# Conv, rank and attention kernel on one core: attention weights on TensorE, two-lane sort, and new written-out orders

## The reference

```python
corr = jnp.einsum('bmc,bnc->bmn', x3, x3) / c
x_sort = jnp.sort(corr, axis=-1)[..., ::-1]
x = x + x_sort[..., ranks]
for window in (4, 16, 32):
    attn = softmax(einsum(q, keys) * scale)
    contexts.append(einsum('blw,blwd->bld', attn, values))
t = t + hidden + (sum(contexts) / 3) @ Wo + bo
```

## Time and profile before

| | |
|---|---|
| time, median of 3 | 4914.16 us (4904.6 to 4914.23) |
| profiled execution, own time | 4910.64 us |
| its span, first to last instruction | 4908.8 us |
| VectorE (DVE) busy | 87% |
| TensorE (PE) busy | 81% |
| ScalarE (ACT) busy | 60% |
| GpSimd (POOL) busy | 18% |
| mean granted TensorE clock | 0.896 of 2.4 GHz |

### The profile page before, as it was taken

How to read it: one execution, slowest core, us unless ns; L and a number is a source line. 1 busy time by engine, 2 the same in 40 slices (tenths; PEclk the granted TensorE clock), 3 DMA queues, 4 the chain that set the end, 5 groups by cost and what they waited for, 6 DMA issues and landing times.

```text
span 4908.8 us, 56286 instructions
## 1 busy us (share of the span) xinstructions
PE 3958.7 (81%) x19410; PEld 2667.5 (54%) x19410; DVE 4267.6 (87%) x5380; ACT 2954.4 (60%) x7241; POOL 884.1 (18%) x580
## 2 busy tenths in 40 slices
PE   5747748889798988989798988989798987867587
PEld 3616424567456654567456654567456654545354
DVE  1098999999999999999999999999999999999521
ACT  4526526687467846687467846677467845554452
POOL 2316000242005300242005300242005300000000
PEclk8878869999799998999799988999799998988798
DMA  4314100232013210232013210232013210010001
GB/s 132 98 35 123 37 0 18 67 105 63 16 43 110 79 36 18 71 104 65 11 43 110 79 36 18 71 102 63 14 44 110 77 34 16 20 30 27 10 24 37
DMA packets 226037, 269.28 MB, mean 55 GB/s; under 512 B 26831, under 2 KB 188506, under 8 KB 225626
## 3 DMA queue, kind: packets, MB, share of 16 engines
q0 software_dynamic: 46080, 151.03, 10.6%
q1 hardware_dynamic: 179674, 114.65, 8.0%
HBM read 242.25 MB, written 23.34 MB: 54 GB/s over the span
## 4 chain that ended last, share of the span: by engine, by line
DVE 41%; PE 36%; ACT 9%; issue 6%; POOL 4%; DMA 4%; SPq 1%; DVEq 0%; POOLq 0%; ACTq 0%
PE bank L597 5%; POOL gath L759 4%; PE bank L1298 3%; PE bank L1633 3%; PE bank L1628 3%; DMA gath<-quads,idx 3%; PE bank L1613 3%; DVE srt_b L794 3%; DVE srt_b L881 3%; DVE srt_b L796 3%; DVE srt_a L893 2%; DVE srt_b L873 2%; DVE srt_a L794 2%; DVE srt_a L796 2%; PE bank L569 2%
## 5 line engine op out<-in xcount | busy, mean ns | idle before, releaser
L759 POOL DMA_INDIRECT gath<-quads,idx x576 | 883.9, 1535 | 3075.4 <-DVE idx L722 1990.3
L597 PE MATMUL bank<-diag,gath 128*128 128x128 f32 x4608 | 615.0, 296 | 168.5 <-DMA gath<-quads,idx 168.5
L639 ACT ACTIVATE diag<-ident,w 128x128 f32<-128x128 f32 x2304 | 704.7, 393 | 30.7 <-DVE w L737 21.2
L597 PEld LDWEIGHTS bank<-diag,gath 128*128 128x128 f32 x4608 | 593.8, 211 | 203.9 <-DMA gath<-quads,idx 187.6
L1613 PEld LDWEIGHTS bank<-e2w,act 128*128 128x128 f32 (+1 forms) x3072 | 408.0, 198 | 161.3 <-issue 156.7
L1628 PE MATMUL bank<-mu_t,e2w 128*128 128x512 f32 (+1 forms) x768 | 421.9, 632 | 82.4 <-DMA e2w<-moe_w_t 36.2
L1633 PE MATMUL bank<-gated_u,e2w 128*128 128x512 f32 (+1 forms) x768 | 426.2, 638 | 36.7 <-DVE act L1713 32.9
L1713 DVE TENSOR_TENSOR act<-act,bank 128x512 f32<-128x512 f32 (+1 forms) x384 | 261.0, 680 | 183.6 <-PE bank L1633 160.8
L1613 PE MATMUL bank<-e2w,act 128*128 128x128 f32 (+1 forms) x3072 | 413.2, 281 | 1.6 <-DVE act L1713 1.6
L1681 ACT ACTIVATE act<-bank 128x512 f32<-128x512 f32 (+1 forms) x384 | 227.6, 593 | 208.6 <-PE bank L1628 206.0
L873 DVE TENSOR_TENSOR srt_b<-srt_a 128x1024 f32<-128x1024 f32 x192 | 350.9, 1828 | 1.5 <-issue 0.3
(11 more groups left out here) (348 smaller groups left out, 8134.4 us busy)
## 6 DMA issues: line engine op xcount, KB each, us to landing
e2w<-moe_w_t SPq DMA_DIRECT2D x256, 170.5 KB
quads<-xn_tok SPq DMA_DIRECT2D x256, 64.0 KB
e1w<-L_ffn_w SPq DMA_DIRECT2D x256, 64.0 KB, 1.9
e2w<-moe_w_t SPq DMA_DIRECT2D x256, 64.0 KB
gath<-quads,idx POOLq DMA_INDIRECT x576
e2w<-moe_w_t SPq DMA_DIRECT2D x128, 42.5 KB
x_tok<-x SPq DMA_DIRECT2D x8, 512.0 KB, 4.4
out<-tm SPq DMA_DIRECT2D x16, 256.0 KB, 2.5
```

Source lines behind the costliest of these rows:

```text
L597: ins = T.matmul(FB[q % 2][:, k * P:(k + 1) * P], gath[:, g % 2, k, s * C:(s + 1) * C], diag[:, g % 2, 4 * k + s], start=(s == 0), stop=(s ...
L639: ins = SC.activation(diag[:, g % 2, n], ident[:], ACT.Copy, scale=w[:, n:n + 1])
L759: pool.indirect_dma_start(gath[:, g % 2, k], None, quads, bass.IndirectOffsetOnAxis(idx[:, TG * g + k:TG * g + k + 1], 0)).then_inc(sem["g ...
```

## The change

- `prob` goes. VectorE takes the reciprocals only. ScalarE builds twelve diagonals `pdiag` (identity scaled by a reciprocal) for a unit, and TensorE multiplies each window's `sm` with its diagonal, three windows into one bank; this transposes and weights at once. The keys of the tile before (32 of them) now lie on partitions 0 to 31, so their values are computed once more on 32 partitions (`v_past`).
- The sort pairs token j with j + 512 and works on two interleaved lanes of 512; each lane has merges of m = 8 (four to a lane) to 1024, all at distance 2 or more, and the last, bitonic merge takes lane 0 against lane 1 backwards. `places` goes. `corr_used` is set after the first full layer.
- The three bias rows are loaded broadcast to 128 partitions and added with the identity as weights.
- The quads are stored in 16 DMAs of 128 KB, each from 32 partitions with the token column as the slowest dimension, once both halves of `xn_tok` are there.
- The order strings of all kinds but `fill` are new. VectorE's letters are the same in number (228 S, 14 F, 36 C in `early`); ScalarE has 2 and TensorE 1 C letter more for each C unit.

```diff
     DVE_early=(
-        "SSSSSSSSSSSSSSSSSSSSSSSSSSSSSSFFSSFSSFSSSSSSSSSSSSSSSFSSSFSSFFSSFSSSSSSSSSSSSSSSSSSSSSSSSSSSSSSS"
-        "SSSSSSSSSSSSSSSSSSSSSSSSSSSCSSCSSSSSSSSSSCCSSCCSSSSSFSSCFSSCFSSFSSSFCSSCSSCSSCSSCSSSCSSSSSSSSSSS"
-        "SSSSCSSCSSSSSSSSSSSCCSSCSSCSSCSSCCSSCSSCSSCSSSSSCSSSSCCSSSSCCSSSSCCSSSSCSSCSSCSSSSSSSS"
+        "SSSSSSSSSSSSSSSSFFSSSFSSFSSSSSSSSSSSSSSSFSSSFSSFFSSFSSSSSSSSSSSSSSSSSSSSSSSSSSSSSSSSSSSSSSSSSSSS"
+        "SSSSSSSSSSSSSSSSSSSSSSSSSSSSSCSSCSSSSSSSSCCSSCSSCSSSSSSSSSSSSCFFSSCFSSFSSCFCSSCSSSCSSCSSCSSSSSSS"
+        "SSSSSSSSSSCSSCSSSSSSSSSSSCSSCSSCSSCSSCSSSCCSSCSSCSSCSSSSCSSSSCCSSSSCCSSSSCCSSSSCSSCSSC"
     ),
...
     PE_full=(
...
-        "MCMCCCCCCCCMCMCMMMMFMMMFMFMMCMMMMFCMMMMMMCFCCFCCFFCCFCFCCFFFFFFFFFFFF"
...
+        "MMCMFMMMFMMFMCMMMFMCMMMFMMMCMMMFCCMMMFFCCMMMFCCMFMFMMMFCMMMFCMMMCMMFFFF"
...
     DVE_full=(
-        "MCMSSCSSMSSSSMSSCCMSSCCMSSMSSMSSSCSSCMSSMSSCMCSSSCMCSSCMCSSMSSSSSSSMSSSSSSSSCMFFCMSSFSSSFSSSSCSS"
...
+        "MCSSCMSSSSSSSMSSSCCMSSCCMSSMSSSMSSMSSSSCSSSCMSSMSSCMCFCFCSSCMCFSSMSSSSSMSSFSSSSSSMSSSSSMSSMSSCSS"
...
             x_in=16, x_t=4, xt_sb=4, gn_mom=4, gn_avg=4, gn_std=2, gn_scale=2, gn_out=6, xn_back=2, xn_tok=2,
-            om_done=2, om_t=2, om_ps=1, om_sb=1, sig=1, quad_out=16 * 32, idx=1, w4=1,
+            om_done=2, om_t=2, om_ps=1, om_sb=1, sig=1, quad_out=16 * 16, idx=1, w4=1,
             gath0=16 * TG * NG // 2, gath1=16 * TG * NG // 2, diag=NG, colt=NG, cols=NG, conv=NT, x1=NT,
-            corr_mm=24, corr_sb=16, sd=1, absd=8, x2_copy=1, out0=16, out1=16, dve_F=17, dve_C0=53, dve_C1=54)
+            corr_mm=24, corr_sb=16, sd=1, absd=8, x2_copy=1, out0=16, out1=16, dve_F=17, dve_C0=47, dve_C1=48)
...
             load(conv_w[:], A["L0_conv_kernel"].rearrange("(t c) f -> c t f", c=C))
-            load(conv_bias[:], A["L0_conv_bias"].rearrange("a b c f -> (a b c) f"))
+            load(conv_bias[:], A["L0_conv_bias"].rearrange("a b c f -> (a b c f)").partition_broadcast(P))
...
         def sp_F(sp, i):
             q = quads.rearrange("(y x) (s c) -> y x s c", x=CELL, c=C)
-            for t in range(NT):
-                if t % 4 == 0:
-                    sp.wait_ge(sem["xn_tok"], img("xn_tok", i, t // 4 + 1))
-                    settle(sp)
...
-                for dy in range(2):
-                    for dx in range(2):
-                        there = q[ROWS * t + 1 - dy:ROWS * t + 1 - dy + ROWS, 1 - dx:1 - dx + WIDTH, 2 * dy + dx]
-                        sp.dma_start(there, xn_tok[:, t]).then_inc(sem["quad_out"], 16)
-                if t % 4 == 3:
-                    yield
+            sp.wait_ge(sem["xn_tok"], img("xn_tok", i, 2))
+            settle(sp)
+            sp.wait_ge(sem["gath0"], img("gath0", i, 0))
+            settle(sp)
+            sp.wait_ge(sem["gath1"], img("gath1", i, 0))
+            settle(sp)
+            for dy in range(2):
+                for dx in range(2):
+                    for r in range(ROWS):
+                        there = q[r + 1 - dy:r + 2 - dy + HEIGHT - ROWS:ROWS, 1 - dx:1 - dx + WIDTH, 2 * dy + dx]
+                        sp.dma_start(there.rearrange("t x c -> x t c"),
+                                     xn_tok[WIDTH * r:WIDTH * (r + 1)]).then_inc(sem["quad_out"], 16)
+                yield
 
...
                     T.matmul(out, ident[:], x_tok[:, t], start=True, stop=False)
-                    T.matmul(out, ones[0:1, :], conv_bias[:], start=False, stop=False)
+                    T.matmul(out, ident[:], conv_bias[:], start=False, stop=False)
                     for k in range(TAPS):
...
                 yield
-                there = corr[:, t % UT].rearrange("p (s k r) -> p s k r", k=2, r=P)
+                there = corr[:, t % UT].rearrange("p (b k w) -> p b k w", k=2, w=2)
-                    SC.activation(there[:, :, k], FB[1 - k][:].rearrange("p (s r) -> p s r", r=P), ACT.Identity,
+                    SC.activation(there[:, :, k], FB[1 - k][:].rearrange("p (b w) -> p b w", w=2), ACT.Identity,
                                   scale=0.5 / C).then_inc(sem["corr_sb"], 1)
                     yield
...
                 lo, hi = src[:, :, 0:size // 2], src[:, :, size // 2:size]
-                if size == TOK:
-                    hi = hi[:, :, ::-1]
 
-            def places(buf):
-                return buf[:].rearrange("p g (s r) -> p g s r", s=8)
...
-
-                V.tensor_tensor(out_lo, lo, hi, ALU.max)
-                yield
-                link.put(V.tensor_tensor(out_hi, lo, hi, ALU.min))
-                yield
-                link.wait()
...
-            m = 16
-            while m < TOK:
-                first = m == 16
-                if not first:
+            ins = yield from compare(8, runs(corr, 8), runs(srt_a, 8))
+            ins.then_inc(sem["corr_used"], 1)
+            yield
+            dve.wait_ge(sem["corr_used"], unit("corr_used", i, h))
+            now = 0
+            m = 8
+            while m <= TOK:
+                if m > 8:
                     link.wait()
-                ins = yield from compare(m, runs(corr if first else bufs[now], m), runs(bufs[1 - now], m))
-                if first:
-                    ins.then_inc(sem["corr_used"], 1)
-                else:
+                    ins = yield from compare(m, runs(bufs[now], m), runs(bufs[1 - now], m))
                     link.put(ins)
-                yield
-                if first:
-                    dve.wait_ge(sem["corr_used"], unit("corr_used", i, h))
-                now = 1 - now
+                    yield
+                    now = 1 - now
                 here, there = runs(bufs[now], m), runs(bufs[1 - now], m)
 
...
                 k = m // 4
-                while k >= 1:
+                while k >= 2:
                     lo, hi = pairs(here, k)
                     out_lo, out_hi = pairs(there, k)
                     link.wait()
                     V.tensor_tensor(out_lo, lo, hi, ALU.max)
                     yield
-                    if k == 1:
-
-                        V.tensor_copy(edges(there, 0, 1), edges(here, 0, 1))
+                    if m == 8:
+
+                        link.put(V.tensor_tensor(hi, lo, hi, ALU.min))
+                        yield
+                        link.wait()
+                        link.put(V.tensor_copy(lo, out_lo))
+                        yield
+                        break
+                    if k == 2:
+
+                        V.tensor_copy(edges(there, 0, 2), edges(here, 0, 2))
                     elif k < m // 4:
 
                         V.tensor_copy(edges(there, 1, k // 2), edges(here, 1, k // 2))
                     link.put(V.tensor_tensor(out_hi, lo, hi, ALU.min))
                     yield
-                    if k == 1:
+                    if k == 2:
                         now = 1 - now
                         break
...
 
-            k = TOK
+            pair = bufs[now][:].rearrange("p g (j w) -> p g j w", w=2)
+            lo, hi = pair[:, :, :, 0], pair[:, :, ::-1, 1]
+            half = bufs[1 - now][:].rearrange("p g (w j) -> p g w j", w=2)
+            link.wait()
+            V.tensor_tensor(half[:, :, 0], lo, hi, ALU.max)
+            yield
+            link.put(V.tensor_tensor(half[:, :, 1], lo, hi, ALU.min))
+            yield
+            now = 1 - now
+            k = TOK // 2
...
             yield
+            pe.wait_ge(sem["qkv_sb"], unit("qkv_sb", i, h, 3))
+            for t in range(UT):
+                ins = T.matmul(CB[0][0:BACK, t * P:(t + 1) * P], utile(t)[:, P - BACK:P], wqkvo[:, 2], start=True, stop=True)
+            ins.then_inc(sem["qkv"], 1)
+            yield
             pe.wait_ge(sem["qkv_sb"], unit("qkv_sb", i, h, 2))
             for p in range(2):
                 for t in range(2):
@@ -1030,27 +1009,28 @@
             for p in range(2):
                 pe.wait_ge(sem["probd"], unit("probd", i, h, p + 1))
                 if p == 0:
-                    pe.wait_ge(sem["prob_z"], unit("prob_z", i, h))
-                    pe.wait_ge(sem["qkv_sb"], unit("qkv_sb", i, h, 3))
-                for t in range(2):
-                    for s in range(2):
-                        ins = T.transpose(CB[p][:, (2 * t + s) * P:(2 * t + s + 1) * P], prob[:, 2 * p + t, s * P:(s + 1) * P], ident[:])
+                    pe.wait_ge(sem["qkv_sb"], unit("qkv_sb", i, h))
+                for t in range(2 * p, 2 * p + 2):
+                    for k, n, at in ((0, BACK, 0), (BACK, P, P)):
+                        for w in range(NW):
+                            ins = T.matmul(CB[p][0:n, t % 2 * 2 * P + at:t % 2 * 2 * P + at + P], sm[:, t, w, k:k + n],
+                                           pdiag[:, t * NW + w], start=(w == 0), stop=(w == NW - 1))
                 ins.then_inc(sem["prob_ps"], 1)
                 yield
...
                     out = CB[2][:, t * P:(t + 1) * P]
-                    past = v_tok[:, t - 1] if t else v_halo[:]
```

(39 more changed lines are left out.)

141 lines of the change are left out of this document (55 added, 86 removed).

## The result

The changed kernel takes 4735.3 us (median of 4 runs, 4731.7 to 4740.5) against 4910.8 for the kernel before on the same chip: ratio 0.9648, 95% interval 0.9636 to 0.966.

What follows compares the result with a forecast made beforehand. VectorE was taken to set the pace except in fill and drain. From 4910.64: fill -4, early body -17, six full bodies and the late one -78.4, drain +5, together -94.4: 4816, stated as 4818 us; range 4775 to 4870.

Steps and rivals of the forecast that it cites:

- A row on one partition costs 0.32 us, its neighbour on 128 partitions 0.31: nothing either way: TensorE's bias matmuls: moving the rows from one to 128 partitions was claimed to change nothing in the time.
- I give the other new orders no gain and no loss: Order strings in the full bodies: an earlier start of F hides behind VectorE, the other new orders change nothing.
- shortens the time by about that much: Bodies 0 to 7: a microsecond taken from VectorE saves about a microsecond, as long as nobody else becomes late.
- slack for 5 us: Full bodies: the attention chain, some 5 us a unit longer, costs nothing, as two C units share 550 us.
- The rival of shorter waits: VectorE's waits in seven bodies: the orders shorten them by 6 us each, 42 more, giving 4776; chance 0.12.
- What hides TensorE's 9.0 is its own idle time: Attention on TensorE: 9.0 us added work an image, mostly hidden; 1.6 us an image charged, bounds 0 and 9.0.
- Drain, +5: Drain: the longer attention chain has no slack there and adds 5 us, bounds 0 and 8.
- VectorE's work: VectorE, per image: sort saves 2.6 us a unit and attention 3.8, together 12.8 us.
- no price for lanes: Sort's last merge: step-of-two reads are free; the rival had 3.3 us more a unit, 4871, chance 0.05.
- Fill: Fill: fewer stores let the first gather go earlier, -5.5, bias rows' loads +1.5; -4, bounds -5.5 and +2.
- late correlations: Rival at seven image borders: new orders make the sort wait for `corr`, 162 us in, 4986; chance 0.06.
- the prediction's other case: Fill's stores: if SBUF ports limit, they take 45 us and the fill is 22 us longer, a sum of 4843.

## Why the prediction was wrong, and where it was right

**The step that failed: "A row on one partition costs 0.32 us, its neighbour on 128 partitions 0.31: nothing either way".** The two means of the earlier trace rows don't hold the price, because it shows in when the matmuls around it start. The runs put 72 us in its place (44 under the old orders): 0.37 to 0.39 us a matmul, 7.1 us of TensorE a full body, 9.4 us of the body. Without it the number would have been near: the changed kernel with the bias rows undone takes 4807 us, where 4818 was said for a term of nothing (own range 4795 to 4840). The comparison with `x_tok` could not warn: its mean is 291 ns in the changed kernel with the rows on 128 partitions and on one, while the bias matmul's goes from 275 to 321 and the eighteen behind it from 275 to 283. It should have gone from start to start, against a matmul of the same columns that has only neighbours of 128 partitions.

**"I give the other new orders no gain and no loss".** That the rest of the sum came out near is luck: two steps of it were wrong by far more than the 11 us that were left. Undoing the orders costs 214 us; under the old strings the attention costs 128 instead of gaining. The stages say so too: with the bias rows undone the six full bodies gave 56 us where 67 were said, and the late one 22 where 11 were (27.5 in the changed kernel). In the full bodies VectorE's idle time then is 24.4 us, 3.6 more than before, where 1.6 were said. The forecast said that a microsecond taken from VectorE "shortens the time by about that much", which for the attention's 3.8 us a unit holds only if other work moves between the reciprocals and the layer norm. It said that the string has "slack for 5 us" for the longer chain in the full bodies; under the old strings it had none. The rival of shorter waits had the right sign (its 6 us a body stand against 5.5 measured) and the wrong cause: without the bias rows on 128 partitions the waits grow. Only on the wait for `dtr` do the orders alone do what it said (3.5 us over the six bodies with the sort and the new orders, 29.7 before), and M's waits grow for it.

**"What hides TensorE's 9.0 is its own idle time".** Under the old orders it did not; under the new ones TensorE has less idle time around the attention and a higher clock. The term itself was too small: the weighting and `v_past` take 152.3 us of records in the whole run of the attention alone, the transposes took 27.3, so 15.6 an image instead of 9.0 (records overlap a little, and part ran at half clock). The bias rows took back 7.1 to 8.9 (busy us a full body, under the new orders and the old).

**Drain, +5.** It became 1 us shorter, but the term was too small, not too large. Counted from the end of VectorE's last addition of sorted ranks, the attention lengthens the drain by 11.1 us under the old orders (322.6 to 333.7) and by 8.2 under the new ones (312.3 with it undone, 320.5), and the new orders shorten it by 10.7 (324.2 to 313.5, with the sort of the changed kernel in both). The bias rows give 1.9. Two errors cancel here: a price of 5 for 8 to 11, and nothing for the orders.

**Right.** VectorE's work: 13.3 us a full body against 12.8 (the sort 4.9, said 5.2; the attention 7.6, said 7.6); the sort's opening 18.32 us, to the hundredth near 18.3, and no price for lanes (that rival is dead). A lone sort gives only 28 us of the 42 that its 2.6 a unit would make in eight bodies, since under the old orders waits take the rest. Fill -5.3 against -4, stores the larger part (4.1 in one execution each). The sum itself has a slip of 2 us: 4816.2 and 3.5 make 4820, not 4818; and the late correlations' 162 us on it make some 4980, not 4986. By an estimate from the Trainium skill (DMA: Bandwidth & Descriptors, Why a DMA increments its semaphore by 16 and not by 1), which has 16 DMA engines at a store instead of 4, the stores would need a quarter of 22.7 us; the trace has 8.5: the direction agrees, the factor is 2.7, and since the stores are also half as many, the run doesn't separate the two. The Trainium skill's rule on ports (SBUF — State Buffer, Door 1: The DMA port swizzle), from which the prediction's other case had 45 us, did not decide here. The late correlations didn't come: after the first sort's 24.2 us all waits of a first compare for `corr` make 0.2 together, and the full bodies are equal within 8 us.

**What stays open.** Which letters of the new strings carry the gain wasn't separated; that M and F fill the attention's wait, and that the clock is higher in the block of unit (i-1,1), is what the rows show, and no single exchange of letters was timed. How the 214 us of the orders divide among less idle time, the clock and the earlier start of F is open too.

## What to carry to other kernels

Price a matmul by the start of the next one, not by its own record, and compare it with neighbours on as many partitions; here a small bias matmul costs TensorE 0.4 us more on 1 or 32 partitions than on 128 with the identity as weights. In a kernel whose engines follow fixed orders, time saved on the pacing engine can turn into a wait: of two savings of VectorE under the same old strings, the sort's 4.9 us a body gave 28 us, the attention's 6.8 cost 128. Look at what the engine does next and who it will wait for. Where TensorE must wait for a dozen us, other matmuls are worth moving there, for the time and, as far as the rows show, for the clock.

## What the runs showed of the hardware

- A matmul (fp32, two records) on 1 or on 32 partitions between matmuls on 128 takes 0.37 to 0.39 us more, start to start and at full clock, than the same on 128 partitions; 1 and 32 don't differ (2.84 and 2.83 us a tile, records of 321 ns each).
- TensorE's clock can eat a saving: with a third of the weighting matmuls after a wait of 11.1 us it was granted 0.50 and the stretch took 18.3 us; with all of them after 12.2 us 0.85 and 16.0 us; with other matmuls in the wait 1.00 and 13.4 us.
- VectorE reads every second element of 2048 at the full rate (2.28 us), where writing every eighth of 1536 took 2.94 us.
